# Two steps' products with v issued as one group, once in sixteen steps

## The reference

```python
q = _apply_rope(proj(Wq, bq), cos, sin) * scale
k = _apply_rope(proj(Wk, bk), cos, sin)
attn = jnp.einsum('bhsd,bhtd->bhst', q, k)
attn = jax.nn.softmax(attn, axis=-1)
out = jnp.einsum('bhst,bhtd->bhsd', attn, v)
x = _layernorm(x + out_proj(out))
x = _layernorm(x + relu(x @ Wq1.T + b1) @ Wq2.T + b2)
```

## Time and profile before

| | |
|---|---|
| time, median of 3 runs | 3215.34 us (3215.28 to 3215.95) |
| span of the profiled execution | 3215.2 us |
| PE busy | 3174.7 us, 99% |
| DVE busy | 2976.8 us, 93% |
| ACT busy | 2522.3 us, 78% |
| POOL busy | 2271.1 us, 71% |
| DMA, mean of 16 engines | about half busy |

### The profile page before, as it was taken

The page is one execution under the profiler, slowest core; times in us unless marked ns, Lnnn a source line. Parts: engine busy times, 40 slices in busy tenths (PEclk is TensorE's granted clock), DMA queues, the critical chain, the costliest instruction groups (busy, mean ns, idle before and its releaser), DMA issues.

```text
span 3215.2 us, 83523 instructions
## 1 busy us (share of the span) xinstructions
PE 3174.7 (99%) x31606; PEld 1763.2 (55%) x31606; DVE 2976.8 (93%) x5711; ACT 2522.3 (78%) x4960; POOL 2271.1 (71%) x2582
## 2 busy tenths in 40 slices
PE   6999999999999999999999999999999999999998
PEld 4445555555555555555555555555555555554555
DVE  7999999999999999999999999999999999999995
ACT  3888888878878878888878878888888878778775
POOL 2576867867767767768768768768678677674556
PEclk7999999999999999999999999999999999999999
DMA  7545355454454454453453453553554544534411
GB/s 205 126 102 113 90 116 113 97 116 111 98 117 107 96 120 105 100 119 100 104 121 96 108 115 94 113 117 92 116 113 96 116 109 99 118 97 86 98 52 49
DMA packets 312717, 342.09 MB, mean 106 GB/s; under 512 B 77372, under 2 KB 259964, under 8 KB 312316
## 3 DMA queue, kind: packets, MB, share of 16 engines
q1 hardware_dynamic: 311740, 335.97, 45.7%
q10 hardware_dynamic: 576, 0.79, 0.2%
HBM read 196.41 MB, written 140.24 MB: 105 GB/s over the span
## 4 chain that ended last, share of the span: by engine, by line
PE 96%; DVE 1%; DMA 1%; ACT 1%; issue 0%; POOL 0%; SPq 0%; ACTq 0%; POOLq 0%; DVEq 0%
PE ob L1089 31%; PE sc L1071 28%; PE job L822 25%; PE ms L1056 11%; PE job L874 0%; ACT prob L1231 0%; DVE mxp L1410 0%; DVE mxp L1663 0%; PE sc L822 0%; DMA qa<-qk_parts 0%; DMA os_<-wv 0%; DMA maxima<-nm 0%; SPq L514 0%; POOL hid_r L1840 0%; DMA qk_parts<-parts 0%
## 5 line engine op out<-in xcount | busy, mean ns | idle before, releaser
L1410 DVE TENSOR_REDUCE mxp<-ms 128x1 f32<-128x512 f32 x4064 | 2601.4, 681 | 178.2 <-PE ms L1056 147.1
L1231 ACT ACTIVATE prob<-sc 128x512 f32<-128x512 f32 x4074 | 2214.4, 598 | 585.4 <-PE sc L1071 557.4
L1056 PE MATMUL ms<-ka,qa 48*128 48x512 f32 x4064 | 1485.3, 436 | 3.0 <-DVE mxp L1663 2.2
L1071 PE MATMUL sc<-qa,ka 50*128 50x512 f32 x4074 | 1476.4, 434 | 3.7 <-DMA qa<-maxima 1.7
L1071 PEld LDWEIGHTS sc<-qa,ka 50*128 50x128 f32 x4074 | 688.3, 184 | 1019.0 <-ACT prob L1231 857.5
L1089 PE MATMUL ob<-prob,v_sb 128*17 128x512 f32 (+1 forms) x8528 | 1086.3, 581 | 1.9 <-ACT at_st L1238 1.4
L1056 PEld LDWEIGHTS ms<-ka,qa 48*128 48x128 f32 x4064 | 689.9, 184 | 7.8 <-DVE mxp L1410 4.8
L442 POOL TENSOR_TENSOR rot<-ev_sb,cs_sb 128x512 f32<-128x512 f32 x60 | 77.1, 1286 | 604.9 <-DVE ev_sb L1451 595.2
L1805 POOL TENSOR_TENSOR hid_r<-hid,hid_r 128x512 fp32r<-128x512 f32 x248 | 319.8, 1289 | 19.8
L1089 PEld LDWEIGHTS ob<-prob,v_sb 128*17 128x17 f32 x8528 | 141.4, 95 | 310.8 <-issue 307.1
L822 PEld LDWEIGHTS job<-h_t,w_sb 64*128 64x128 f32 x3968 | 270.4, 185 | 16.9 <-issue 1.0
(11 more groups left out here) (260 smaller groups left out, 2914.7 us busy)
## 6 DMA issues: line engine op xcount, KB each, us to landing
qk_parts<-parts SPq DMA_DIRECT2D x122, 512.0 KB, 4.3
ka<-qk_parts SPq DMA_DIRECT2D x378, 128.0 KB, 4.7
qa<-qk_parts SPq DMA_DIRECT2D x378, 128.0 KB, 7.4
attention<-at_st SPq DMA_DIRECT2D x127, 256.0 KB, 3.4
v_sb<-v_ones SPq DMA_DIRECT2D x68, 272.0 KB, 8.5
v_ones<-v_st SPq DMA_DIRECT2D x64, 272.0 KB, 2.4
xn<-x SPq DMA_DIRECT2D x63, 256.0 KB, 8.9
out<-y SPq DMA_DIRECT2D x63, 256.0 KB, 3.0
```

The lines of the kernel that those rows point to most:

```text
L1056: nc.tensor.matmul(ms[upto(b, g, NS1, at) % MS_BANKS][:, :], operand(qa, b, unit_, j, ROWS)[:, qt * P:(qt + 1) * P], operand(ka, b, unit_, ...
L1071: nc.tensor.matmul(score_bank(upto(b, g, HG * STEPS, n))[:, :], operand(ka, b, unit_, head, ROWS + MROWS)[:, tt * P:(tt + 1) * P], operand ...
L1231: nc.scalar.activation(prob[st_ % 2][:, head_at(b, g, st_, j), :], score_bank(upto(b, g, HG * STEPS, n))[:, :], ACT.Exp).then_inc(s["exp_d ...
L1410: nc.vector.reduce_max(mxp[(b * G + g) % 2][:, kh, j * TT + qt:j * TT + qt + 1], ms[upto(b, g, NS1, at) % MS_BANKS][:, :], AX.X).then_inc( ...
```

## The change

At step 12 of every unit of all batches but the last, the groups of steps 10 and 11 are issued one behind the other, between the two pairs of heads. Step 11 then has no group: its job stays where it was, or, where there is none, its pairs of heads follow each other. The group of step 10 thus reads its probabilities while those of step 12 are written, so there are three `prob` buffers, used by the step's running number. Their space comes from `parts`, which now lies in the fourth q slot.

```diff
+PROBS = 3
+JOINED = (12,)
-def behind_last_pair(jobs):
-    return len(jobs) == 1 and jobs[0][2] in JOBS_BEHIND
+def joined(b, st_):
+    return b < B - 1 and st_ in JOINED
+def behind_last_pair(b, st_, jobs):
+    return joined(b, st_) or joined(b, st_ + 1) and len(jobs) == 0 or len(jobs) == 1 and jobs[0][2] in JOBS_BEHIND
+def step_number(b, g, st_):
+    return (b * G + g) * STEPS + st_
+def weighed_at(b, g, st_):
+    now = step_number(b, g, st_)
+    if now == 0 or joined(b, st_ + 1):
+        return []
+    before = now - (2 if joined(b, st_) else 1)
+    return [(n // (G * STEPS), n // STEPS % G, n % STEPS) for n in range(before, now)]
...
-        parts = sb("parts", [P, 2, 2, PARTS, TQ], fp32r)
+        parts = qa[RING][:, :, :].rearrange("p h t -> p (h t)").rearrange("p (i e a t) -> p i e a t", i=2, e=2, a=PARTS)
-        prob = [sb(f"prob{i}", [P, HG, NQ]) for i in range(2)]
+        prob = [sb(f"prob{i}", [P, HG, NQ]) for i in range(PROBS)]
...
-                    last = nc.tensor.matmul(ob[32 * j:32 * j + VW, begin:end], v_sb[values][:, tt, j, :], prob[st_ % 2][:, j, begin:end],
+                    last = nc.tensor.matmul(ob[32 * j:32 * j + VW, begin:end], v_sb[values][:, tt, j, :],
+                                            prob[step_number(b, g, st_) % PROBS][:, j, begin:end],
...
-                            if jobs and j == (1 if behind else 3):
-                                weigh_before(b, g, st_, first, 0, NQ)
-                            elif not jobs and j % 2 == 1:
-                                weigh_before(b, g, st_, first, j // 2 * (NQ // 2), (j // 2 + 1) * (NQ // 2))
+                            if (jobs or len(due) != 1) and j == (1 if behind else 3):
+                                for at in due:
+                                    weigh(*at)
+                            elif not jobs and len(due) == 1 and j % 2 == 1:
+                                for at in due:
+                                    weigh(*at, j // 2 * (NQ // 2), (j // 2 + 1) * (NQ // 2))
...
-                if j == 0 and not (b == 0 and g == 0 and st_ < 2):
-                    act.wait_ge(s["pv_done"], upto(b, g, STEPS, st_ - 1))
+                if j == 0:
+                    wait_used(act, s["pv_done"], step_number(b, g, st_) + 1 - PROBS)
```

More of the change, by code:

```diff
@@ L1092, in weigh @@
                     last.then_inc(s["pv_done"], 1)
[L1094 to L1099, removed]
             def run(job_, free):
@@ L1119, in batch @@
                         jobs = jobs_at(b, g, st_, tail)
-                        behind = behind_last_pair(jobs)
+                        behind = behind_last_pair(b, st_, jobs)
+                        due = weighed_at(b, g, st_)
                         tiles = [maximum_tiles(b, g, 4 * st_ + n, last) for n in range(4)]
@@ L1227, in exps @@
                 act.wait_ge(s["s2_ready"], upto(b, g, HG * STEPS, n + 1))
-                if j == 0 and not (b == 0 and g == 0 and st_ < 2):
-                    act.wait_ge(s["pv_done"], upto(b, g, STEPS, st_ - 1))
-                nc.scalar.activation(prob[st_ % 2][:, head_at(b, g, st_, j), :], score_bank(upto(b, g, HG * STEPS, n))[:, :], ACT.Exp
+                if j == 0:
+                    wait_used(act, s["pv_done"], step_number(b, g, st_) + 1 - PROBS)
+                nc.scalar.activation(prob[step_number(b, g, st_) % PROBS][:, head_at(b, g, st_, j), :], score_bank(upto(b, g, HG * STEPS, n))[:, :], ACT.Exp
                                      ).then_inc(s["exp_done"], 1)
@@ L1330, in batch @@
                             taken = [(b + (g - 1) // G, (g - 1) % G, 1)]
-                        in_pieces = jobs_at(b, g, 1, tail) and not behind_last_pair(jobs_at(b, g, 1, tail))
+                        in_pieces = jobs_at(b, g, 1, tail) and not behind_last_pair(b, 1, jobs_at(b, g, 1, tail))
                         for at in taken:
```

## The result

| | before | after |
|---|---|---|
| time, median of 4 runs each | 3215.31 us (3213.99 to 3215.95) | 3263.82 us (3261.18 to 3266.35) |
| ratio, 95% interval | | 1.0153 [1.0141, 1.0165] |
| span of the profiled execution | 3215.2 us | 3264.5 us |

The account below looks back on a forecast made before the run. PE's instruction order was taken to bound the kernel: 58 units at 0.80 us (46.4) plus 1.0 for two units without a job, buffers and q slot 0, on 3215.3 gave 3262.7 us; range 3250 to 3274.

Parts of the forecast that it names:

- the second rival: No difference: the loss is given back later in the unit, where PE would have waited anyway; 3215 to 3222 us, chance 0.06.
- The wait in place of the group: Step 11 without its product group: scores wait for ACT's exponentials to empty their banks; 0.80 us per unit, 58 units, 46.4 us.
- A1: Start of the score of head 3 of step 11; its exponential was forecast to end 1.66 us after A0.
- A0: Start of the score of head 2 of step 11, the point from which the forecast counts its times.
- B0: Start of the score of head 0 of step 12, forecast to wait for A0's exponential, until A0 + 1.23 us.
- B1: Start of the score of head 1 of step 12, forecast to wait for A1's exponential, until A0 + 1.71 us.
- W10: Product group of step 10, moved to step 12; forecast to start 0.43 us behind B1, at A0 + 2.14.
- W11: Product group of step 11; forecast to start 0.88 us behind W10, with 0.98 from it to C0.
- C0: Start of the score of head 2 of step 12; forecast at A0 + 4.00 us, where the old order had 3.20.
- The weights that load late: At B1: a held score's weights load only at its release, so W10 follows by 0.43 us, not 0.33.
- The first rival: Faster: exponentials are in time and only the change of matmul kind goes; 17.4 us saved, 3197.9 us, chance 0.06.
- The two units without a job: Third and fourth unit of batch 0, no job at steps 11 and 12: DVE decides, +0.5 us each, 1.0 us together.

Follow-up runs that it names:

- Both short: Changed kernel, step 11 exponentials of heads 2 and 3 over 8 columns, maximum reductions over 64, exponentials scaled by 0: joined 3221.07 us, base (not joined) 3212.49 us.

## Why the prediction was right

*What bounds it* held: PE's order sets the time, and a hole in it is not given back (the second rival). In steps 0 to 10 and 13 to 15 no step of the middle units is more than 0.03 us longer or shorter than before.

*The wait in place of the group* was the term that decided, and each part of it was measured: A1's exponential at A0 + 1.65 (1.66 forecast), release 0.06 (0.05), B0 at 1.22 (1.23), B1 at 1.71 (1.71), W10 0.43 behind it, W11 and C0 another 1.84 (1.86). A0 to C0 is 3.98 where 4.00 was forecast, so 0.79 a unit. Two of the experiments agree: without the joining the loss is gone, with a second joining it comes again.

*The weights that load late* (0.43, not 0.33): the trace agrees with the earlier trace rows. The Trainium skill's rule of weight loads pulled ahead (page "TensorE: Matmul & The Clock Gate", table of specifications) is not seen for a score that is held: W10 stands 0.43 behind B1.

*DVE* I had called not late. True in the changed kernel, where B1 comes at A0 + 1.71 and the reduction ends at 1.30; the run with short exponentials shows it releasing B1's tile at A0 + 1.35. It was the next wait in line, and a forecast of a cheaper ACT without it (0.03 to 0.10 instead of 0.43) was wrong.

*The first rival*, that the joining pays if the exponentials are in time, needed B1 by A0 + 0.91. With exponentials of 0.17 us B0 alone comes at 0.80 and B1 0.33 behind, at 1.13: with two banks even these do not reach it. By the rows one change of kind is saved, an estimate of 0.3 us as in the forecast, and one hole is paid; no run shows the saving by itself.

*The two units without a job* were the term mis-sized: 0.5 each, measured 1.04 where the clock stays and 2.65 where it falls. That DVE decides there was right, but it runs dry for 1.21 us where the clock stays, and I had put 0.8 as the most. I had priced a fall of the clock at nothing and named it as a sign of being wrong; in the profiled execution, the longest of the four, it makes 3.2 us of the 49.3 between the spans. It did not move the forecast much since two units are few, and an earlier first score (1.9 us in this trace, and it moves by some 4 us from trace to trace) took part of it away.

That the sum came within 1.1 us of the median is therefore in part luck. In the profiled execution the 58 units make 46.0 us (46.4 forecast) and the two others 5.3 (1.0), less 1.9 for the start. The term that carries the forecast is right by itself; the small ones were off and partly cancel.

*Buffers and q slot*: 0, measured as a ratio of 1.0001 [0.9991, 1.0010].

## What to carry to other kernels

Work between a producer and its consumer on one engine is cover for whatever the other engines do there; before moving it, follow each bank that the next instructions need, take the release that comes last, and then the one behind that. Joining groups saves a change of matmul kind (by estimate 0.3 us here) only if what stood between them isn't needed as cover: two banks and a score-to-release time of 1.2 us asked for more than that. An experiment that gives "no change" in total may still have moved the wait: read the step it was aimed at before calling the theory false.

## What the runs showed that I had not expected

The granted clock fell to 0.50 in a kernel that is busy 98% of its span, behind two steps in which PE had only scores with holes between; in another execution with the same order in these units it stayed at 1.00 and the units were 1.6 us shorter, and in a third it fell in one of the two and not in the other. What decides between the two is open: filling the hole kept 1.00 in one profile, but so did one without the filling, so the part of the hole is not shown.

A third score bank is worth more than the 17.4 us that the joining had by the first rival: with short reductions, three of them made the kernel 68 us faster than before, as holds of 0.25 us in steps 3, 5 and 7 went. Short reductions without the third bank gave 2.4 us (the base of *Both short*, where some exponentials were short too), so nearly all of it is the bank. With full reductions and only two banks for the maximum tiles the kernel was 290 us slower.
